# Moving sixteen low-part subtractions from VectorE to GpSimd, and powers by column at the end, in a two-layer graph kernel

## What is computed

```python
h = relu(A @ (x @ W1) + b1)
h = relu(A @ (h @ W2) + b2)
x = layernorm(x + h)
f = (A @ x @ V1 + A @ A @ x @ V2 + A @ A @ A @ x @ V3) / 3
x = layernorm(x + f)
```

## Time and profile before

| what | value |
|---|---|
| median of three runs | 256.37 us |
| the profiled execution, its own time | 256.48 us |
| its span | 254.7 us |
| TensorE (PE) busy | 247.2 us, 97% |
| VectorE (DVE) busy | 200.9 us, 79% |
| ScalarE (ACT) busy | 193.1 us, 76% |
| GpSimd (POOL) busy | 16.7 us, 7% |
| mean granted TensorE clock | 0.999 |

### The profile page before, as it was taken

The page is one execution under the profiler, slowest core; times in us unless marked ns, Lnnn a source line. Parts: engine busy times, 40 slices in busy tenths (PEclk is TensorE's granted clock), DMA queues, the critical chain, the costliest instruction groups (busy, mean ns, idle before and its releaser), DMA issues.

```text
span 254.7 us, 3758 instructions
## 1 busy us (share of the span) xinstructions
PE 247.2 (97%) x1152; PEld 204.3 (80%) x1152; DVE 200.9 (79%) x391; ACT 193.1 (76%) x337; POOL 16.7 (7%) x24
## 2 busy tenths in 40 slices
PE   8999999999999999999999999999999999999991
PEld 8688788888888888877888888888888888888880
DVE  0898899796789889898778777767676767888844
ACT  2897998886868787978877787867677776788751
POOL 1000000000003021130000000000000000303032
PEclk9999999999999999999999999999999999999999
DMA  6999999920000000000000000000000000010111
GB/s 213 389 386 385 387 386 387 400 91 0 0 3 3 0 0 3 0 0 1 0 4 0 0 0 3 0 0 1 4 0 0 0 3 0 0 42 0 45 41 42
DMA packets 11396, 20.49 MB, mean 80 GB/s; under 512 B 1264, under 2 KB 2288, under 8 KB 11248
## 3 DMA queue, kind: packets, MB, share of 16 engines
q1 hardware_dynamic: 11088, 19.93, 21.4%
q10 hardware_dynamic: 288, 0.33, 0.4%
HBM read 19.20 MB, written 1.05 MB: 80 GB/s over the span
## 4 chain that ended last, share of the span: by engine, by line
PE 82%; SPq 5%; DMA 4%; DVE 3%; ACT 2%; issue 2%; POOL 0%; POOLq 0%; DVEq 0%; ACTq 0%
PE filters L393 17%; PE filters L386 17%; PE filters L387 17%; PE pair L393 9%; PE pair L386 9%; PE pair L387 9%; DMA adj<-a_t 4%; SPq L271 3%; PE weighted L361 2%; PE turned L363 2%; ACT ring_high L517 2%; DVE ring_low L632 1%; SPq L269 1%; SPq L275 1%; DVE operand_low L586 1%
## 5 line engine op out<-in xcount | busy, mean ns | idle before, releaser
L632 DVE TENSOR_TENSOR ring_low<-adj,ring_high 128x512 fp32r<-128x512 f32 x240 | 160.0, 688 | 34.8 <-ACT ring_high L517 32.0
L517 ACT ACTIVATE ring_high<-adj 128x512 fp32r<-128x512 f32 x240 | 148.6, 629 | 32.7 <-PE filters L387 15.9
L386 PE MATMUL filters<-ring_high,operand_low 128*128 128x512 f32 x156 | 62.0, 398 | 0.0
L393 PE MATMUL filters<-ring_low,operand_high 128*128 128x512 f32 x156 | 61.2, 392 | 0.4 <-DVE ring_low L632 0.4
L387 PE MATMUL filters<-ring_high,operand_high 128*128 128x512 f32 x156 | 60.8, 390 | 0.0
L393 PEld LDWEIGHTS filters<-ring_low,operand_high 128*128 128x128 f32 x156 | 29.3, 188 | 8.0 <-DVE ring_low L632 1.8
L387 PEld LDWEIGHTS filters<-ring_high,operand_high 128*128 128x128 f32 x156 | 29.3, 188 | 5.7
L386 PEld LDWEIGHTS filters<-ring_high,operand_low 128*128 128x128 f32 x156 | 29.3, 188 | 5.7
L386 PE MATMUL pair<-ring_high,operand_low 128*128 128x512 f32 x84 | 33.3, 396 | 0.0
L393 PE MATMUL pair<-ring_low,operand_high 128*128 128x512 f32 x84 | 33.1, 394 | 0.2
L387 PE MATMUL pair<-ring_high,operand_high 128*128 128x512 f32 x84 | 32.7, 390 | 0.0
(11 more groups left out here) (84 smaller groups left out, 209.0 us busy)
## 6 DMA issues: line engine op xcount, KB each, us to landing
adj<-a_t SPq DMA_DIRECT2D x48, 256.0 KB, 9.6
resident_raw<-a_t SPq DMA_DIRECT2D x16, 256.0 KB, 9.7
nodes<-x_rows SPq DMA_DIRECT2D x1, 1024.0 KB, 11.6
lead<-lead_in SPq DMA_DIRECT2D x3, 256.0 KB, 4.7
out_rows<-nodes SPq DMA_DIRECT2D x3, 256.0 KB, 2.4
lead<-lead_in ACTq DMA_DIRECT2D x1, 192.0 KB, 2.9
lead<-lead_in SPq DMA_DIRECT2D x1, 128.0 KB, 2.7
lift_raw<-lifts SPq DMA_DIRECT2D x1, 128.0 KB, 11.3
```

Of the source, the lines that this page charges most:

```text
L386: nc.tensor.matmul(bank, y_low, a_high, start=first, stop=False)
L393: used = nc.tensor.matmul(bank, y_high, a_low, start=False, stop=last)
L517: nc.scalar.activation(ring_high[:, n % RING, :], source, ACT.Copy).then_inc(high_ready, 1)
L632: nc.vector.tensor_tensor(ring_low[:, n % RING, :], source, ring_high[:, n % RING, :].bitcast(F32), ALU.subtract).then_inc(low_ready, 1)
```

## The change

1. The sixteen `resident_low` subtractions of hop 0 leave VectorE's order. GpSimd does them, in the same order of tiles, ahead of all its powers; each waits for its `resident_high`. They write to the same place, and TensorE's wait (`resident_low_ready`) is the same.
2. At the end there are two halves in place of three pieces. TensorE loads the residual of tiles 0 and 1 and of tile 2, adds the sums of tiles 0 and 1, and only then loads the residual of tile 3 and adds the sums of tiles 2 and 3. VectorE takes statistics by half. GpSimd raises four single columns. VectorE normalises all four tiles, in place of two; ScalarE normalises none. SyncE's queue stores tiles 0 and 1 (128 KB), ScalarE's queue tiles 2 and 3 (128 KB).

```diff
@@ gpsimd
+            for hop, c, k in tile_order(0):
+                if not streamed(k):
+                    j = k // (STREAMED + 1)
+                    pool.wait_ge(resident_high_ready, residents(c, k))
+                    nc.gpsimd.tensor_tensor(resident_low[:, c, j, :], resident_raw[:, c, j, :],
+                                            resident_high[:, c, j, :].bitcast(F32), ALU.subtract
+                                            ).then_inc(resident_low_ready, 1)
...
-            for piece, part in enumerate(PIECES):
-                pool.wait_ge(variance_ready, whole_groups * HALVES + piece + 1)
-                nc.gpsimd.tensor_tensor(rstd[:, part], variance[:, part], exponent[:, part], ALU.pow
-                                        ).then_inc(rstd_ready, 1)
+            for half, part in enumerate(halves):
+                pool.wait_ge(variance_ready, whole_groups * HALVES + half + 1)
+                for t in range(part.start, part.stop):
+                    nc.gpsimd.tensor_tensor(rstd[:, t:t + 1], variance[:, t:t + 1], exponent[:, t:t + 1], ALU.pow
+                                            ).then_inc(rstd_ready, 1)
@@ tensor
+            nc.tensor.matmul(weighted[:, 0:half_tiles, :], ident[:], first_half, start=True, stop=False)
+            nc.tensor.matmul(last_banks[2], ident[:], nodes[:, TILES - 2, :], start=True, stop=False)
+            pe.wait_ge(chunk_evacuated, HOPS * CHUNKS)
+            add_sums(0)
+            add_sums(1).then_inc(post_multiplied, 1)
+            nc.tensor.matmul(last_banks[3], ident[:], nodes[:, TILES - 1, :], start=True, stop=False)
+            pe.wait_ge(chunk_evacuated, HOPS * CHUNKS + 1)
+            add_sums(2)
+            add_sums(3).then_inc(post_multiplied, 1)
@@ scalar
-            act.wait_ge(shift_ready, whole_groups * HALVES + 1)
-            for t in range(half_tiles):
-                nc.scalar.activation(nodes[:, TILES - TPC + t, :], weighted[:, t, :], ACT.Identity, bias=shift[:, t:t + 1],
-                                     scale=rstd[:, t:t + 1]).then_inc(normalised, 1)
...
+            act.wait_ge(last_normalised, TPC)
+            act.dma_start(out_rows[:, last_tiles(1), :], nodes[:, last_tiles(1), :]).then_inc(out_stored, 16)
@@ vector
-                elif hop == 0:
-                    dve.wait_ge(resident_high_ready, residents(c, k))
-                    nc.vector.tensor_tensor(resident_low[:, c, j, :], resident_raw[:, c, j, :],
-                                            resident_high[:, c, j, :].bitcast(F32), ALU.subtract
-                                            ).then_inc(resident_low_ready, 1)
...
+            for half in range(HALVES):
+                dve.wait_ge(post_multiplied, HOPS * CHUNKS + half)
+                norm_stats(hop, c, half, last_banks[halves[half]])
+                norm_moments(hop, c, half)
+            for t in range(TPC):
+                dve.wait_ge(rstd_ready, whole_groups * HALVES + t + 1)
+                nc.vector.tensor_scalar(nodes[:, TILES - TPC + t, :], last_banks[t],
+                                        moments[:, t, 0:1], rstd[:, t:t + 1], ALU.subtract, ALU.mult
+                                        ).then_inc(last_normalised, 1)
```

More of the change, by code:

```diff
@@ L98 @@
 WIDELY = {"stats": (2, 6), "moments": (4, 8), "shift": (6, 10), "apply": (7, 8, 11, 12), "high": 13, "low": 15}
-PIECES = (slice(0, 2), slice(2, 3), slice(3, 4))
 OVERHANG = 12
@@ L232, in residuals, with last_tiles @@
             return NORMED.index(hop) * CHUNKS + c + 1
[L234 to L242, removed]
+        def last_tiles(half):
+            return slice(TILES - TPC + half * half_tiles, TILES - TPC + (half + 1) * half_tiles)
+        last_banks = [weighted[:, 0, :], weighted[:, 1, :], turned[:, 0, :], pair[:, 0, 0:D]]
         def half_of(hop, c, half):
@@ L291, in _ @@
                 sp.dma_start(out_rows[:, tiles, :], nodes[:, tiles, :]).then_inc(out_stored, 16)
[L292 to L297, removed]
+            sp.wait_ge(last_normalised, half_tiles)
+            sp.dma_start(out_rows[:, last_tiles(0), :], nodes[:, last_tiles(0), :]).then_inc(out_stored, 16)
+            sp.wait_ge(out_stored, 16 * (CHUNKS - 1 + HALVES))
         @block.gpsimd
@@ L428, in _, with add_sums @@
             pe.wait_ge(residual_added, residuals(HOPS - 1, CHUNKS - 2))
[L429 to L436, removed]
+            def add_sums(t):
+                return nc.tensor.matmul(last_banks[t], chunk_t[:, t * P:(t + 1) * P], ident[:], start=False, stop=t > 0)
+            first_half = nodes[:, last_tiles(0), :]
+            nc.tensor.matmul(weighted[:, 0:half_tiles, :], ident[:], first_half, start=True, stop=False)
[7 more added lines that the diff above has]
+            add_sums(3).then_inc(post_multiplied, 1)
         @block.scalar
@@ L531, in _ @@
                                      ).then_inc(chunk_evacuated, 1)
-            act.wait_ge(shift_ready, whole_groups * HALVES + 1)
-            for t in range(half_tiles):
-                nc.scalar.activation(nodes[:, TILES - TPC + t, :], weighted[:, t, :], ACT.Identity, bias=shift[:, t:t + 1],
-                                     scale=rstd[:, t:t + 1]).then_inc(normalised, 1)
-            tiles = last_tiles(0)
-            act.wait_ge(normalised, whole_groups * TPC + half_tiles)
-            act.dma_start(out_rows[:, tiles, :], nodes[:, tiles, :]).then_inc(out_stored, 16)
+            act.wait_ge(last_normalised, TPC)
+            act.dma_start(out_rows[:, last_tiles(1), :], nodes[:, last_tiles(1), :]).then_inc(out_stored, 16)
         @block.vector
@@ L552, in norm_stats @@
                 for t in range(half_tiles):
-                    last = nc.vector.bn_stats(stats[:, half * half_tiles + t, :], rows[:, t, :])
+                    last = nc.vector.bn_stats(stats[:, half * half_tiles + t, :], rows[t])
                 last.then_inc(stats_ready, 1)
@@ L605, in visits @@
                         dve.wait_ge(residual_added, residuals(hop, c))
-                        norm_stats(hop, c, half, nodes[:, first:first + half_tiles, :])
+                        norm_stats(hop, c, half, [nodes[:, first + t, :] for t in range(half_tiles)])
                     for hop, c in norms(n, "moments", half):
@@ L634, in _ @@
                     n += 1
-                elif hop == 0:
-                    dve.wait_ge(resident_high_ready, residents(c, k))
-                    nc.vector.tensor_tensor(resident_low[:, c, j, :], resident_raw[:, c, j, :],
-                                            resident_high[:, c, j, :].bitcast(F32), ALU.subtract
-                                            ).then_inc(resident_low_ready, 1)
             for n in range(ITEMS, ITEMS + OVERHANG):
                 visits(n)
-            done = HOPS * CHUNKS - 1
@@ L645, in _ @@
[L645 to L659, removed]
@@ L660, in _ @@
-            norm_shift(HOPS - 1, CHUNKS - 1, 0)
-            for piece in range(1, len(PIECES)):
-                t = PIECES[piece].start
-                dve.wait_ge(rstd_ready, whole_groups * HALVES + piece + 1)
-                nc.vector.tensor_scalar(nodes[:, TILES - TPC + t, :], piece_bank(piece)[:, 0, :], moments[:, t, 0:1],
-                                        rstd[:, t:t + 1], ALU.subtract, ALU.mult).then_inc(last_normalised, 1)
+            hop, c = HOPS - 1, CHUNKS - 1
+            for half in range(HALVES):
+                dve.wait_ge(post_multiplied, HOPS * CHUNKS + half)
+                norm_stats(hop, c, half, last_banks[halves[half]])
+                norm_moments(hop, c, half)
```

## The result

The changed kernel takes 258.38 us (median of 4 runs, 258.07 to 258.59), the kernel before 256.36 us: a ratio of 1.0084, 95% interval 1.007 to 1.0097. It is 2.0 us slower. I had forecast slower with 260.8 us, in a range of 256.4 to 263.0. The direction held, and so did the mechanism in the main; the size was forecast at + 4.4 us, and + 2.0 is less than half of that. The changed kernel's own profiled execution took 258.07 us with a span of 256.1 us.

The account below looks back on a forecast made before the run. TensorE was taken to bound hop 0, with VectorE near behind; exclusion would cost + 4.2 us there and the end + 0.2, so 256.4 + 4.4 = 260.8 us, range 256.4 to 263.0 (the forecast's own from 258.1).

Parts of the forecast that it names:

- What bounds the kernel: Hop 0: TensorE at its peak, 2.72 us per four tiles; VectorE needs 2.41, so has 0.31 us to spare.
- Exclusion: Hop 0: VectorE and GpSimd wait for each other's SBUF reads, so their times add; chance 0.72 with subtraction 0.95 us or more.
- A: Hop 0: no exclusion for long operations, GpSimd's 1.23 us fit beside VectorE's 1.81; time 256.5 us; chance 0.21.
- B: Hop 0: no exclusion, and relieved VectorE also removes TensorE's waits, at most 2.4 us; time 255.4 us; chance 0.04.
- C: Hop 0: GpSimd gets its turn only when the ring is full and TensorE stands still; + 18 us, 275 us; chance 0.03.
- The sum of part 1: Hop 0: stretch costs 1.81 plus 1.23, 3.04 us against 2.72; 15 stretches lose 4.8, posts return 0.6, net + 4.2 us.
- The bound from which there is a loss: Hop 0: a GpSimd subtraction loses time only from 2.72 - 1.81 + 0.04 = 0.95 us each.
- The Trainium skill's price for the subtraction: Hop 0, GpSimd's subtraction: 2.2 ns an element, 1.12 us for 512; hop 0 loses 2.6 us, time 259.2 us.
- The posts' slack: Three posts inside hop 0: TensorE spends 0.81 us on each, VectorE 0.60, so 0.6 us is given back.
- catches up after each disturbance: Hop 0: with 0.31 us to spare in each 2.72, VectorE recovers after each disturbance.
- Part 2: End of program: four 0.55 us powers start the last normalisation 0.18 us later, store even; + 0.2 us, ends 0 and + 0.5.
- Handover at nothing: Hop 0, between VectorE and GpSimd: handover costed at nothing; 0.05 us a stretch would add 0.8 us.

Follow-up runs that it names:

- e5_pairs: Kernel before plus nine small GpSimd and VectorE phases behind its last store; in phase 6 GpSimd's addition of a constant, beside four VectorE subtractions, lasted 3.07 us.
- the repeat: The changed kernel run once more, unaltered: 258.20 us, ratio 1.0091 against the kernel before.
- e3_half: Kernel before with every second resident low part (eight of sixteen) made by GpSimd, old end kept: 256.69 us, ratio 1.0013.
- e4_spare: Kernel before, VectorE making all low parts, plus sixteen GpSimd subtractions into a scratch tile nobody reads: 261.81 us, ratio 1.022.

## Why the prediction was right and wrong

**What bounds the kernel: right.** TensorE's peak was the bound of hop 0, and VectorE had 0.31 us to spare in 2.72.

**Exclusion: right.** I read it from the ends of two powers. The rows of pairs show it directly, and rivals A (no exclusion), B (faster) and C (VectorE always first) fall with them: GpSimd's subtractions got their turn behind the VectorE subtraction that was running. One GpSimd operation of another kind didn't (phase 6 of e5_pairs). By its own terms A's time was 256.4 + 0.2 = 256.6 us, not 256.5.

**The sum of part 1: this is the step that failed.** I wrote that "a stretch of four tiles costs VectorE 3 x 0.60 = 1.81 us plus GpSimd's 1.23". GpSimd's price came out right, 1.23 us from three small rows against 1.26 measured, but in part by luck: the same rows give 0.10 + 512 x (0.83 + 0.69) = 0.88 us for an operation with one input, and the addition of a constant took 1.50. What was wrong is that VectorE waits for the whole of it. It is held up for 1.11 us. A stretch costs 0.60 + 0.60 + 1.71 = 2.91 us, and the loss in it is 0.19 us, not 0.32. Where the loss is the small difference of two large numbers, 0.12 us too much in the 1.23 took it up by two thirds: 15 x 0.19 - 0.6 = 2.3 us in place of 4.2, against 1.95 to 2.9 measured, by which profiles are compared. The bound from which there is a loss, 0.95 us, speaks of the held-up time, and so does the range's end.

The Trainium skill (SBUF — State Buffer, SBUF: two separate sides) has the lock held for the whole instruction. The runs agree on who excludes whom. They differ on how long: VectorE was held up for 1.11 of GpSimd's 1.26 us, and for 0.42 of 1.50 us with one input, and once a whole VectorE addition (267.05) ran between two that one GpSimd addition held up.

The Trainium skill's price for the subtraction (GPSIMD Engine Reference, Elementwise — side-by-side cycle accounting) gave, from 4497 ns for 2048 columns, an estimate of 1.12 us. Being scaled down, it holds only a quarter of what is fixed in an instruction, and the durations here are some 0.19 us and 2.1 ns a column. So it was too low for the instruction's 1.26 us, and met the held-up 1.11 by luck. The 259.2 us worked out from it were the nearest number in the prediction.

**The posts' slack: about right.** I gave back 0.6 us for three posts. By the chunk, TensorE has 11.78 - 4 x 2.72 = 0.9 us for a post and what follows it and VectorE 0.60 for the operand, so 0.9 us for three. That would leave 15 x 0.19 - 0.9 = 1.9 us; measured were 2.16, 1.95 and, in the repeat, 1.9.

**The start of hop 0: a term left at nothing.** That agreement is partly luck, since two things that the sum lacks nearly cancel. The sum has each stretch alike. The chunks from the second on do run as it says, 12.20 to 12.25 us against 11.78, so + 0.45 each. The first sixteen steps take 13.61, 13.34 and 13.35 us in the three profiles of this kind, against 11.99 to 12.17 where VectorE makes all low parts: 1.2 to 1.6 us more. And the profile before has 0.6 us in its second sixteen that the changed kernel has not. That VectorE "catches up after each disturbance" follows from its 2.41 us against 2.72; at 2.91 against 2.72 it can't. In the first sixteen steps TensorE's weight loads wait 1.9 us for VectorE's ring parts and 1.1 us for GpSimd's resident ones, where they waited 1.0 and 0.6 us for VectorE's. How much of the first sixteen's loss is the hold-up and how much the late resident parts wasn't tried; e3_half, where TensorE waited for no GpSimd part, had 12.88 us, so 0.7 to 0.9 of it need no late part.

**Part 2: too high.** The forecast was + 0.2 us with 0 and + 0.5 as ends; alone it measured - 0.2, with no change just inside the interval. The sum gave four powers 0.55 us each and a little between, 249.52 to 251.76, so 2.24 us; from start to start they are 0.52, 2.09 us in all, so the last normalisation starts 0.03 us later, not 0.18. And "I take this as even" of the store was unfounded: the tail behind the last normalisation is 2.7 to 2.95 us in the profiles with the new end and 3.0 to 3.7 in those with the old.

**Handover at nothing: not contradicted.** The 1.11 us are read from start to start and hold any handover there is, so the runs don't give it a price of its own.

The range was right to reach down to 256.4, but the forecast's own, from 258.1, left only 0.3 us below the result. In the range of 1.05 to 1.33 us for GpSimd I had varied the price and not the share of it that VectorE feels.

## What to carry to other kernels

Before work is moved to an idle engine, ask what that engine shares with the one it is taken from. Here a subtraction of 0.60 us was exchanged for a hold-up of 1.11, and the idle engine was no help at all. In these runs the exchange cost nothing where VectorE's subtraction had an operand in PSUM, and next to nothing once VectorE had slack for the difference (e3_half behind its first sixteen steps); and with a loss that is the difference of two nearly equal rates, each term has to be known to some per cent, since the result multiplies the error. Two single profiles can differ by 1 us in a part that the edit doesn't touch, so compare the parts one by one, over several profiles.

## What the runs showed of the hardware beyond that

- GpSimd's fp32 operation with two inputs of 128 rows takes 0.73, 1.26 and 2.34 us for 256, 512 and 1024 columns. With one input and a constant it took more, 1.50 us for 512 (0.85 for 256), but held a VectorE subtraction up for 0.42 us only.
- Reading one tensor twice into bf16 held VectorE up for 0.84 us, reading two into fp32r for 1.11. Which of the two differences does it wasn't tried.
- GpSimd's memset of 512 columns took 0.52 us and held up nothing.
- A VectorE subtraction that reads PSUM and SBUF ran beside GpSimd's at its own speed (0.67 and 0.68 us), and hid 0.60 us of the 0.84 that the next one would have been held up (e4_spare).
